# POOL copies index columns one at a time, each ahead of its own gather, in the preparation and in the two source stages of a four-layer graph network

## What is computed

```python
edge_index = jnp.stack([src, dst])
h = jnp.maximum(_layernorm(x, axis=-1), 0.0)
x = x + _L0_gnn_ref(h, edge_weight, edge_index, 2)      # two hops: x = segment_sum(w * x[src], dst)
h = jnp.maximum(_layernorm(x, axis=-1), 0.0)
x = x + _L1_gnn_ref(h, edge_index, L1_gnn_W, L1_gnn_b)  # normalised graph convolution
h = jnp.maximum(_layernorm(x, axis=-1), 0.0)
x = x + _L2_gnn_ref(h, edge_index, L2_gnn_W1, L2_gnn_b1, L2_gnn_W2, L2_gnn_b2)
h = jnp.maximum(_layernorm(x, axis=-1), 0.0)
x = x + _L3_gnn_ref(h, src, dst, edge_attr_32, L3_gnn_mW1, L3_gnn_mb1, L3_gnn_mW2, L3_gnn_mb2, L3_gnn_uW1, L3_gnn_ub1, L3_gnn_uW2, L3_gnn_ub2)  # message and update MLPs
```

## Time and profile before

| | |
|---|---|
| three executions | 5804.32 us median (5786.72 to 5818.43) |
| profiled execution | span 5754.7 us; it has no time of its own beside the span |
| median less that span | 49.6 us |
| busy in the span | PE 65%, PEld 52%, DVE 53%, ACT 35%, POOL 58% |
| POOL instructions counted as work | 2843 |
| the 14-column copies, L925 | 62 |
| mean granted TensorE clock | 0.722 |
| chain of waits, largest named shares | PE 2%, another core or an unknown queue 1%, DVE 1% |

### The profile page before, as it was taken

How to read it: one execution, slowest core, us unless ns; L and a number is a source line. 1 busy time by engine, 2 the same in 40 slices (tenths; PEclk the granted TensorE clock), 3 DMA queues, 4 the chain that set the end, 5 groups by cost and what they waited for, 6 DMA issues and landing times. The chain is left out here.

```text
span 5754.7 us, 60611 instructions
## 1 busy us (share of the span) xinstructions
PE 3759.0 (65%) x18706; PEld 3006.2 (52%) x18706; DVE 3033.3 (53%) x7288; ACT 2016.3 (35%) x5132; POOL 3313.7 (58%) x2843
## 2 busy tenths in 40 slices
PE   3776666676999975565556777763566655666665
PEld 2544444446898964444445555553454444455454
DVE  4644444455556546665665766755454434455442
ACT  2444444451111113443444444431233333333332
POOL 4888888887888874444332554553444554445544
PEclk7776666675555557887888777875778877777787
DMA  8333333334444432222222333333121111121110
GB/s 293 51 51 51 51 51 51 51 42 73 87 81 87 87 40 82 78 93 79 96 77 75 108 125 123 112 107 130 54 91 55 59 57 57 54 91 55 60 54 21
DMA packets 335488, 452.10 MB, mean 79 GB/s; under 512 B 208111, under 2 KB 233301, under 8 KB 334740
## 3 DMA queue, kind: packets, MB, share of 16 engines
q1 hardware_dynamic: 159268, 361.69, 17.8%
q0 software_dynamic: 176000, 87.72, 12.5%
HBM read 258.41 MB, written 225.53 MB: 84 GB/s over the span
## 5 line engine op out<-in xcount | busy, mean ns | idle before, releaser
L929 POOL DMA_INDIRECT ga<-table,isl x784 | 783.9, 1000 | 278.1 <-issue 231.3
L1059 POOL DMA_INDIRECT out_x<-acc,osl x392 | 430.0, 1097 | 755.6 <-DVEq L80 640.4
L997 POOL DMA_INDIRECT xu<-acc,osl x392 | 625.1, 1595 | 144.6 <-issue 103.1
L1205 PE MATMUL tp<-xw,cc 128*128 128x394 f32 x784 | 411.5, 623 | 345.8 <-DVE cc L2011 215.4
L1242 PE MATMUL tp<-us,wide 128*128 128x64 f32 x1568 | 416.8, 422 | 87.4 <-DVE us L2139 49.2
L929 POOL DMA_INDIRECT ga<-xu,isl x392 | 394.0, 1005 | 121.5 <-issue 116.5
L1205 PEld LDWEIGHTS tp<-xw,cc 128*128 128x128 f32 x784 | 141.5, 220 | 603.1 <-issue 325.4
L1093 PE MATMUL mm<-ident,wide 128*128 128x128 f32 x1176 | 213.1, 343 | 355.6 <-DVE wide L2218 275.7
L1242 PEld LDWEIGHTS tp<-us,wide 128*128 128x128 f32 x1568 | 380.0, 332 | 92.2 <-DVE us L2139 49.4
L1255 PE MATMUL tp<-acc,wide 128*128 128x64 f32 x1560 | 423.3, 427 | 0.8
L1093 PEld LDWEIGHTS mm<-ident,wide 128*128 128x128 f32 x1176 | 180.0, 182 | 406.1 <-issue 323.2
(11 more groups left out here) (378 smaller groups left out, 9513.8 us busy)
## 6 DMA issues: line engine op xcount, KB each, us to landing
wide<-xu SPq DMA_DIRECT2D x84, 448.0 KB
zx<-key_rows SPq DMA_DIRECT2D x28, 896.0 KB
out_x<-wide SPq DMA_DIRECT2D x56, 448.0 KB, 3.4
table<-acc SPq DMA_DIRECT2D x56, 448.0 KB, 2.5
xf<-xs SPq DMA_DIRECT2D x56, 448.0 KB
wide<-table SPq DMA_DIRECT2D x56, 448.0 KB
xu<-in_x SPq DMA_DIRECT2D x25, 1000.0 KB
hop_even<-zeros SPq DMA_DIRECT2D x1, 12544.0 KB
```

What stands on the lines that cost most here:

```text
L929: nc.gpsimd.indirect_dma_start(o[:, g, :], None, table, bass.IndirectOffsetOnAxis(idx[:, g:g + 1], 0)).then_inc(s, 16)
L997: nc.gpsimd.indirect_dma_start(xu, bass.IndirectOffsetOnAxis(osl[b][:, g:g + 1], 0), acc[b][:, g, :], None, compute_op=ALU.add).then_inc(f ...
L1059: nc.gpsimd.indirect_dma_start(out, bass.IndirectOffsetOnAxis(osl[b][:, g:g + 1], 0), acc[b][:, g, :], None, bounds_check=nodes_max, oob_i ...
L1205: f.key_row.raise_by(nc.tensor.matmul(tp[1][:, at:at + KEYS], reach[:, g * P:g * P + P], key_steps, start=True, stop=True), ("g", b, g))
```

## The change

Where POOL fills the slot, it now copies one column, waits for that copy, issues that column's gather, and goes on to the next column. The semaphore value is counted on through all stages in `copied`. Which rows are gathered, in which order and into what, stays the same; so do the waits for DVE ahead of each unit. Hop 0 after its first four units, hop 1 and the last stage (whose first two copies stay 14 columns wide) keep their code, but for the value that those two copies wait for.

```diff
+            def gather_by_column(o, table, slot, index, c, s, copied):
+
+                for g in range(G):
+                    slot_copy(slot[:, g:g + 1], index[:, c + g:c + g + 1])
+                    after.wait_ge(s_slot, copied + g + 1)
+                    gather(o, table, slot, s, (g,))
+                return copied + G
...
             for u in range(4):
-                slot_copy(isl_of[u][:, :], dstc_i[:, u * G:u * G + G])
-                after.wait_ge(s_slot, base + u + 1)
-                gather(ga_of[u], x, isl_of[u], f.got[u])
-            base += 4
+                copied = gather_by_column(ga_of[u], x, isl_of[u], dstc_i, u * G, f.got[u], copied)
...
-                        slot_copy(isl[b][:, :], index[:, bass.ds(ecol(i, b), G)])
-                        after.wait_ge(s_slot, base + 2 * i + n + 1)
-                        gather(ga[b], table, isl[b], f.got[b])
+                        copied = gather_by_column(ga[b], table, isl[b], index, ecol(i, b), f.got[b], copied)
```

More of the change, by code:

```diff
@@ L930, in gather @@
                         o[:, g, :], None, table, bass.IndirectOffsetOnAxis(idx[:, g:g + 1], 0)).then_inc(s, 16)
+            def gather_by_column(o, table, slot, index, c, s, copied):
[4 more added lines that the diff above has]
+                return copied + G
             after.wait_ge(s_node, 1)
-            base = 0
+            copied = 0
             hop_max, all_max = pool.to_reg(ROWS + 4 * P - 1), pool.to_reg(ROWS + N + 4 * P - 1)
@@ L1014, in _, with body @@
                         after.wait_ge(sp_[0].kept[b], 2 * 16 * STEPS)
-                def body(i, first):
-                    for n, b in enumerate(B2K if k == 0 else B2K[::-1]):
+                def body(i, first, copied):
+                    for b in B2K if k == 0 else B2K[::-1]:
                         if not first:
@@ L1023, in body @@
                                 after.wait_ge(*f.ga_free.at(i - 1, ("g", b)))
-                        slot_copy(isl[b][:, :], index[:, bass.ds(ecol(i, b), G)])
-                        after.wait_ge(s_slot, base + 2 * i + n + 1)
-                        gather(ga[b], table, isl[b], f.got[b])
+                        copied = gather_by_column(ga[b], table, isl[b], index, ecol(i, b), f.got[b], copied)
+                    return copied
                 for i in range(STEPS):
-                    body(i, i == 0)
-                base += 2 * STEPS
+                    copied = body(i, i == 0, copied)
                 for b in B2K:
@@ L1048, in t_gather @@
                         slot_copy(isl[b][:, :], ptr_i[:, bass.ds(tcol(i, b), G)])
-                        after.wait_ge(s_slot, base + b + 1)
+                        after.wait_ge(s_slot, copied + b + 1)
                     gather(ga[b], tables[1], isl[b], tt.got_a[b])
```

## The result

| | before | changed |
|---|---|---|
| median of 4 executions each | 5811.38 us (5786.72 to 5827.10) | 5359.99 us (5359.24 to 5361.50) |
| ratio | | 0.9226, 95% interval 0.92 to 0.9252 |
| profiled span | 5754.7 us | 5358.7 us |
| mean granted TensorE clock | 0.722 | 0.742 |

A forecast was written before the change was run, and what follows sets the result against it. It took POOL to bound hop 0, with POOL waiting for DVE in the source stages. Terms 4.4 + 0 + 3 + 0 = 7.4, say +8 us, on the median 5804.32 gave 5812 us, range 5786 to 5834.

The forecast's parts named there:

- rival 3: Source stages: gathers 1.44 instead of 1.26 us apart crowd DMA engines less, 0 to 5 us gained; 5774 us, chance 0.05.
- the sum: Whole kernel: 4.4 + 0 + 3 + 0 = 7.4, say +8 us, on the median 5804.32, giving 5812 us.
- One more copy: Preparation and source steps: each added copy with its wait costs POOL 0.18 us; 780 copies, 140 us of POOL's time.
- Copies held by DVE: Source steps: DVE's two-input work delays each copy by 0.15 us, 4.2 us a step (bound 8.7 and 10.1).
- Source steps, the cover: Common source steps: 8.9 us added at the last gather, hidden by 20.8 us (stage 0) or 25.2 us (stage 1).
- rival 1: Source steps: copies stand behind DVE's two-input work, each held 0.91 us more, outlasting the cover; 6006 us, chance 0.04.
- Preparation: Before hop 0: POOL's four units end 9.4 us later, within a cover of 40.1 us, so 0 us added.
- Rival 2: Preparation: held copies or queued gathers make hop 0 start late, 20 us, 5832 us; chance 0.08 with partial forms.
- Last step of stage 1 and DVE held: Last gather of stage 1 late, +4.4 us (0.2 to 10.3); copies holding DVE over 28 steps, 3 us (0 to 16).
- The signs: If right: 842 copies, POOL busy 100 to 260 us more, source gathers 1.4 to 1.8 us apart, common-step readers without waits.

The follow-up runs named there:

- e4: Against the kernel before: seven columns copied, waited for and gathered without a break, then the other seven; 4623.68 us beside 4623.33 us, ratio 1.0003.
- e1: Against the kernel before: only source stage 0 gathers by column, preparation and source stage 1 unchanged; 4662.11 us beside 4623.33 us, ratio 1.0089.
- e5: The changed kernel itself run once more, against the kernel before; 4711.79 us beside 4620.26 us, ratio 1.0201.
- e2: Against the kernel before: one 14-column copy kept, a wait already reached added ahead of each gather; 4624.71 us beside 4623.33 us, ratio 1.0003.

## Why the prediction was wrong

**The step that failed** is rival 3: "no reader waits for a gather there, so 0 to 5 us can come of it". It counted only what waits for a gather's data. The gathers' own pace held up engines that wait for none of them, and breaking it gave 225 + 188 + 7 = 420 us. So the sum held the present length of the stages as given, and put at nothing what the change does to it. The rows for it were there. Of the preparation I wrote "after that unit DVE is idle for 28.24 us up to 89.86, for something else than gathers"; it ended by "remote", and POOL was in an unbroken run of gathers until 98; in the changed kernel DVE has no such idle time and runs L2014 from 58.22 on. In the earlier trace rows DVE and PE were busy 21 and 20 of 38 us while POOL gathered; I used that to bound how often a copy meets DVE and did not ask why engines with a full list of work were half idle.

**One more copy** (0.18 us a column): right. In the changed kernel gathers stand 1.44 to 1.45 us apart in most steps, against 1.25.

**Copies held by DVE** (0.15 us each): right in size, 0.09 and 0.13 us. The copies took 109.4 us for 392 in stage 0 and 124.4 us for 391 in stage 1, 0.28 and 0.32 us each against 0.19 undisturbed; some took up to 1.135 us. Of the 784 copies 145 took over 0.3 us, and 144 of these began while DVE ran an instruction with two SBUF inputs. The rule of the Trainium skill (SBUF — State Buffer, "Who interferes with whom") agrees again, at a tenth to a seventh of the full hold of 0.91 us.

**Source steps, the cover** (20.8 and 25.2 us): wrong in kind. That cover was the stall. In both ways, once it is gone, DVE does wait for gathers in common steps: 49.0 us in 13 waits in stage 1 and 31.2 us in 9 in stage 0 of the changed kernel. In the short way POOL's slack was some 4 to 5 us a step (39 to 41 us from first to last gather in steps of 44 to 45, in e4), and the added 6 to 8 us a step went onto the path: 39 us in stage 0 (e1, e5) and 44 in stage 1. This is **rival 1** in its place and effect, POOL's added time beyond the cover, but by a small cover, not by held copies.

**Preparation** (0): hop 0 began at 131.40, not 138. The cover of 40.1 us held the copies, but DVE's sums came 7 us earlier. **Rival 2**, hop 0 late, did not come; in the short way e5 has it at 132.97 against 131.40 in e4, 1.6 us late.

**Last step of stage 1 and DVE held** (4.4 + 3 us): too small to be seen beside the rest.

**The signs.** Copies 842, POOL's busy time up by 262 us (100 to 260 named) and the distance of 1.44 to 1.8 us came nearly as written. POOL's waits for DVE fell by 308 and 322 us a stage instead of 8 to 15 us a step (some 200 at most), and the readers `L2244` and `L2227` (now L2247 and L2230), which I had said would not wait, wait: that was among my signs of being wrong.

**The sum**, +8 us, would have been wrong in the short way too: e5 is 92 us above its kernel before.

## What to carry to other kernels

Idle time that ends by "remote" or "issue" on an engine with its operands ready is a finding, not background: look what another engine does from its start to its end, and whether it ends with it. An unbroken run of indirect DMAs may slow engines that use none of their data, and then spreading it out can give more than it costs; where no such stall is in the trace, the same spreading costs its full time as soon as POOL has no slack. So measure such a change on more than one occasion, and beside the old kernel each time.

## What was not expected of the hardware

- In the long way POOL's indirect DMAs 1.25 us apart hold up PE and DVE (in the step at 2247 us from about the 16th of them on), and in the last stage PE then starts one instruction each 1.4 us. At 1.45 us apart there is no stall, at 1.33 a part of it (medians of a step; the means are 1.30 to 1.41 us in unbroken steps and 1.54 to 1.81 in steps by column). With 64 rows instead of 128 it is the same. What handles one DMA in about 1.4 us isn't shown; that it is such a rate at all is inferred from these numbers.
- Hops 0 and 1 take nearly the same in both ways (the changed kernel begins hop 1 at 1359 us long and 1353 short). There an add-scatter takes POOL 1.6 us itself, so the DMAs stand 1.69 us (hop 0) and 1.92 us (hop 1) apart on average, which fits the distance.
- The long way goes with missing event records: 27,500 to 34,200 landings in every long trace, 55,770 to 55,940 in every short one, while instructions and DMA packets are complete (335,488 packets for the kernel before and for e2). The kernel before (long) lacks 35% of e2's landings in hop 0, where nothing stalls, 63% in source stage 0 and 57% in the last stage; the changed kernel, against e5, lacks 33% in stage 0, where the stall is gone, and 57% in the last, where it is not. So records are lost in any stretch of the long way, and more where it stalls. All executions that are told of here were recorded by the profiler, so it stays open whether the stall exists without recording. The Trainium skill (NOTIFIC — the notification-queue block, "Overflow: three behaviours, one of which stalls the engine") says that this block can drop records or hold up the engine that makes them, depending on its settings. Lost events beside complete instruction records and stalled engines would fit that; no run here shows it, and none was made without recording.
